# A graph layer with two hand-written orders: bucket ranks spread between the chunks of h, zero writes two per chunk, and a new order inside each unit of 20

## What is computed

```python
h = x @ W_in2f
Wij = (ssp(f_ij @ W_filt1 + b_filt1) @ W_filt2 + b_filt2) * rcut_ij[:, None]   # ssp: softplus - ln 2
agg = segment_sum(h[idx_j] * Wij, idx_i, num_segments=6250)
out = layernorm(x + ssp(agg @ W_out1 + b_out1) @ W_out2 + b_out2)
```

## Time and profile before

| | us |
|---|---|
| median of 3 runs | 2242.66 |
| lowest and highest run | 2235.79 and 2242.95 |
| time of the profiled execution | 2232.01 |
| its span, first to last instruction | 2230.1 |
| start of TensorE's first edge layer (line 1768) | 110.04 |
| first and last scatter (line 716) | 135.3 and 2138.7 |
| busy in the span: TensorE, VectorE, GpSimd, ScalarE | 2044.0, 1889.0, 1747.9, 1591.8 |

### The profile page before, as it was taken

One profiled execution on the slowest core, in us unless ns is written; L12 is line 12 of the kernel. 1 busy time (PEld: TensorE's weight loads), 2 busy tenths in 40 slices (PEclk: granted clock), 3 DMA queues, 4 the chain that ended last, 5 costly groups with the idle time before them and its releaser, 6 DMA issues.

```text
span 2230.1 us, 54072 instructions
## 1 busy us (share of the span) xinstructions
PE 2044.0 (92%) x15953; PEld 1681.7 (75%) x15953; DVE 1889.0 (85%) x3919; ACT 1591.8 (71%) x3812; POOL 1747.9 (78%) x1078
## 2 busy tenths in 40 slices
PE   3479999999999999999999999999999999999945
PEld 2357878787878778877878887788878787878733
DVE  6468989898989889988989898898989898989836
ACT  0278777777777777877778777777777777778616
POOL 2048888888888888888888888888888888888873
PEclk9589999999999999999999999999999999999978
DMA  6746666666666665656666656656666666666494
GB/s 234 279 85 104 94 94 96 101 101 88 99 99 89 98 98 94 95 90 106 98 90 100 95 93 100 99 94 94 97 100 97 91 100 96 92 97 96 55 234 128
DMA packets 353785, 239.34 MB, mean 107 GB/s; under 512 B 86919, under 2 KB 332786, under 8 KB 353338
## 3 DMA queue, kind: packets, MB, share of 16 engines
q0 software_dynamic: 146736, 66.85, 32.2%
q1 hardware_dynamic: 196326, 152.61, 27.1%
q10 hardware_dynamic: 10476, 16.77, 2.0%
HBM read 147.25 MB, written 88.83 MB: 106 GB/s over the span
## 4 chain that ended last, share of the span: by engine, by line
DMA 35%; PE 23%; POOL 16%; issue 15%; DVE 5%; ACT 3%; POOLq 0%; ACTq 0%; DVEq 0%; SPq 0%
DMA table<-total,index 33%; POOL table L716 16%; PE unit_psum L1824 6%; PE unit_psum L1843 4%; PE both_psum L1781 4%; PE total_psum L1794 3%; PE pre_psum L1768 2%; PE both_psum L1806 1%; PE both_psum L1777 1%; DMA h_parts<-h_out 1%; DMA b_o<-in_b_o 1%; ACT out_rows L1082 1%; ACT total L852 1%; DVE scat_hot L1377 1%; DVE route_hot L1360 1%
## 5 line engine op out<-in xcount | busy, mean ns | idle before, releaser
L716 POOL DMA_INDIRECT table<-total,index x1019 | 1689.2, 1658 | 428.9 <-issue 255.5
L1824 PE MATMUL unit_psum<-moving,route_hot 128*128 128x258 f32 x3808 | 602.7, 297 | 9.1 <-ACT ring L893 5.8
L1824 PEld LDWEIGHTS unit_psum<-moving,route_hot 128*128 128x128 f32 x3808 | 496.2, 191 | 72.3 <-ACT ring L893 51.4
L893 ACT ACTIVATE ring<-unit_psum 128x258 fp32r<-128x258 f32 x952 | 353.4, 394 | 245.6 <-PE unit_psum L1824 227.2
L869 ACT ACTIVATE h_dst<-both_psum,cols 128x128 f32<-128x128 f32 x1564 | 445.0, 373 | 96.5 <-PE both_psum L1806 95.1
L1843 PE MATMUL unit_psum<-scat_hot,ring 64*128 64x448 f32 x3808 | 461.1, 379 | 10.5 <-DVE scat_hot L1377 6.3
L1377 DVE TENSOR_SCALAR scat_hot<-node_iota,ring 128x448 fp32r<-128x448 uint16 x952 | 433.0, 474 | 9.1 <-ACT ring L893 5.0
L1781 PEld LDWEIGHTS both_psum<-w_f,hidden 128*128 128x128 f32 x3128 | 423.7, 196 | 11.6
L1781 PE MATMUL both_psum<-w_f,hidden 128*128 128x128 f32 x3128 | 421.6, 278 | 0.0
L1360 DVE TENSOR_SCALAR route_hot<-node_iota,cols 128x896 fp32r<-128x896 uint16 x544 | 378.9, 715 | 45.2 <-PE unit_psum L1824 44.2
L1843 PEld LDWEIGHTS unit_psum<-scat_hot,ring 64*128 64x128 f32 x3808 | 340.1, 185 | 89.3 <-ACT ring L893 30.3
(11 more groups left out here) (118 smaller groups left out, 1507.4 us busy)
## 6 DMA issues: line engine op xcount, KB each, us to landing
dst_b<-dst SPq DMA_DIRECT2D x391, 128.0 KB
src_b<-src SPq DMA_DIRECT2D x255, 128.0 KB, 3.4
f_t<-in_f_t SPq DMA_DIRECT2D x100, 256.0 KB, 3.6
table<-total,index POOLq DMA_INDIRECT x1019
table<-zeros ACTq DMA_DIRECT2D x20, 640.0 KB, 5.6
window<-h_parts SPq DMA_DIRECT2D x391, 32.0 KB
parts<-table SPq DMA_DIRECT2D x48, 256.0 KB, 5.0
h_parts<-h_out SPq DMA_DIRECT2D x12, 384.0 KB, 5.4
```

The lines of the kernel that those rows point to most:

```text
L716: pool.indirect_dma_start(tables[table], bass.IndirectOffsetOnAxis(index[:, i, k:k + 1], 0), total[:, i, k, 0:DIM], None, compute_op=ALU.a ...
L893: act.activation(ring[:, r[1] % RING, k, :], unit_psum[:, k % 2, 0:MOVING], ACT.Copy).then_inc(ring_done, 1)
L1824: last = pe.matmul(unit_psum[:, k % 2, 0:MOVING], route_hot[:, tile, k * P:(k + 1) * P], moving[:, tile, :], start=(tile == 0), stop=(tile ...
```

## The change

On all engines the loop over two chunks is unrolled, and the work on the routed edges stands between the chunks: on VectorE the bucket marks stand between chunks 1 and 4, the ranks between chunks 4 and 10, and `judge_windows` stands after the last subtraction of the high part, at the end. `count_in_buckets` is cut into one step per bucket, placed between the `node_features` of chunks 3 to 12. The diagonal of the triangular matrix `earlier` now holds 1024, so that an edge's own count carries a mark; a rank is then `max(rank, counts - 1024)`, one instruction per bucket in place of a product and a sum. SP issues the first loads of features, `dst` and `src` between the stores of h, and ScalarE writes two zeros after each of the chunks 2 to 6, one before each of the chunks 7 to 11, and one before each of the chunks 0 to 2. In the third stage VectorE takes `norm_shift` ahead of the clamp. In the second stage the same steps stand in another order on TensorE, ScalarE and VectorE; a unit now begins and ends about one pair of groups earlier in the pipeline. GpSimd's scatters are unchanged.

```diff
@@ SP
-            for quad in range(FEEDS):
-                load_features((0, quad))
-            sp.wait_ge(edges16_stored, 32)
-            for i in range(QUAD):
-                load_dst((0, i))
-                if plain(i):
-                    load_src((0, i), plain)
-
-            with sp.Fori(0, FULL_CHUNKS // 2 - 1) as j:
-                for b in range(2):
-                    load_x_t((j, b + 2), CHUNK // P)
-                    store_h((j, b), CHUNK // P)
+            for c in range(FULL_CHUNKS - 2):
+                load_x_t((0, c + 2), CHUNK // P)
+                store_h((0, c), CHUNK // P)
+                if 1 <= c <= FEEDS:
+                    load_features((0, c - 1))
+                if c == FEEDS:
+                    sp.wait_ge(edges16_stored, 32)
+                if FEEDS <= c < FEEDS + QUAD:
+                    load_dst((0, c - FEEDS))
+                    if plain(c - FEEDS):
+                        load_src((0, c - FEEDS), plain)
...
@@ GpSimd
             pool.affine_select(out=earlier[:, :], in_=earlier[:, :], compare_op=ALU.is_ge, fill=0.0, base=-1,
+                               pattern=[[1, P]], channel_multiplier=-1).then_inc(const_step, 1)
+            pool.wait_ge(const_step, 3)
+            pool.affine_select(out=earlier[:, :], in_=earlier[:, :], compare_op=ALU.not_equal, fill=OWN_MARK, base=0,
                                pattern=[[1, P]], channel_multiplier=-1).then_inc(consts_made, 1)
...
@@ ScalarE, split_h
-                if not isinstance(c[0], int):
-                    for k in range(1 + b, TABLES, 2):
-                        zero(k, c[0])
-                else:
-                    zero(0, min(2 + c[1], FIFTHS - 1))
+                if c[1] < FIFTHS - 2:
+                    zero(0, 2 + c[1])
+                elif 7 <= c[1] < 7 + FIFTHS:
+                    zero(2, c[1] - 7)
                 act.wait_ge(h_mm, after_chunk(c))
...
                 act.activation(h_out[:, b, 0:tiles, 1, :], h_rest[:, b, 0:tiles, :], ACT.Copy).then_inc(h_mid, 1)
-
-            run_chunks(act, split_h, LAST_H)
+                if 2 <= c[1] < 2 + FIFTHS:
+                    act.wait_ge(edges16_stored, 32)
+                    zero(1, c[1] - 2)
+                    zero(3, c[1] - 2)
+
+            for c in range(FULL_CHUNKS):
+                split_h((0, c), CHUNK // P)
+            split_h((0, FULL_CHUNKS), LAST_H // P)
...
@@ VectorE, ranks
-                for b in range(BUCKETS):
-                    dve.wait_ge(meta_mm, b + 1)
-                    part = rank[:, 0:ROUTES * TILES] if b == 0 else rank_part[:, :]
-                    counts = (both_psum if b % 2 else unit_psum)[:, :, 0:META_HALF * TILES]
-                    dve.wait_ge(meta_step, steps)
-                    dve.tensor_tensor(part.rearrange("p (h c) -> p h c", h=2), counts,
-                                      in_bucket[:, b, :].rearrange("p (h c) -> p h c", h=2), ALU.mult
-                                      ).then_inc(meta_step, 1)
-                    steps += 1
-                    if b:
-                        dve.wait_ge(meta_step, steps)
-                        dve.tensor_tensor(rank[:, 0:ROUTES * TILES], rank[:, 0:ROUTES * TILES], rank_part[:, :],
-                                          ALU.add).then_inc(meta_step, 1)
-                        steps += 1
+            def rank_in_bucket(b):
+                dve.wait_ge(meta_mm, b + 1)
+                counts = (both_psum if b % 2 else unit_psum)[:, :, 0:META_HALF * TILES]
+                ranks = rank[:, 0:ROUTES * TILES].rearrange("p (h c) -> p h c", h=2)
+                if b == 0:
+                    dve.tensor_scalar(ranks, counts, -OWN_MARK, 0.0, ALU.add, ALU.max).then_inc(meta_step, 1)
+                else:
+                    dve.wait_ge(meta_step, META_HOTS + b)
+                    dve.scalar_tensor_tensor(ranks, counts, -OWN_MARK, ranks, ALU.add, ALU.max).then_inc(meta_step, 1)
...
@@ VectorE, chunks of h (take_hi and take_mid are the two subtractions of split_h)
-            run_chunks(dve, split_h, LAST_H)
+            full = CHUNK // P
+            take_hi((0, 0), full)
+            make_order()
+            take_mid((0, 0), full)
+            take_hi((0, 1), full)
+            find_buckets()
+            take_mid((0, 1), full)
+            for b in range(4):
+                mark_bucket(b)
+            take_hi((0, 2), full)
...
+            take_mid((0, 3), full)
+            find_local()
+            take_hi((0, 4), full)
+            rank_in_bucket(0)
+            take_mid((0, 4), full)
+            rank_in_bucket(1)
+            rank_in_bucket(2)
+            for c in range(5, 11):
+                take_hi((0, c), full)
+                rank_in_bucket(2 * c - 7)
+                take_mid((0, c), full)
+                if c < 10:
+                    rank_in_bucket(2 * c - 6)
+            place_routed()
+            take_hi((0, 11), full)
+            make_biases()
+            take_mid((0, 11), full)
+            take_hi((0, FULL_CHUNKS), LAST_H // P)
+            judge_windows()
+            take_mid((0, FULL_CHUNKS), LAST_H // P)
...
@@ TensorE, chunks of h
-            run_chunks(pe, node_features, LAST_H)
+
+            for c in range(4):
+                node_features((0, c), CHUNK // P)
+            count_in_bucket(0)
+            count_in_bucket(1)
+            node_features((0, 4), CHUNK // P)
+            node_features((0, 5), CHUNK // P)
+            count_in_bucket(2)
+            node_features((0, 6), CHUNK // P)
+            for c in range(7, FULL_CHUNKS):
+                count_in_bucket(2 * c - 11)
+                count_in_bucket(2 * c - 10)
+                node_features((0, c), CHUNK // P)
+            for b in range(2 * FULL_CHUNKS - 11, BUCKETS):
+                count_in_bucket(b)
+            node_features((0, FULL_CHUNKS), LAST_H // P)
+            count_crowded()
...
@@ VectorE, last_layers
             def last_layers(i):
+                c = plus(i, -2)
+                if is_chunk(c):
+                    b, tiles = c[1] % 2, tiles_of(c)
+                    dve.wait_ge(e_inv, after_chunk(c))
+                    previous(dve, e_norm, c, after_chunk)
+                    dve.scalar_tensor_tensor(norm_shift[:, b, 0:tiles], mean_var[:, b, 0:tiles, 0], -1.0,
+                                             inv_dev[:, b, 0:tiles], ALU.mult, ALU.mult).then_inc(e_shift, 1)
+
                 c = i
...
-                c = plus(i, -2)
-                if is_chunk(c):
-                    b, tiles = c[1] % 2, tiles_of(c)
-                    dve.wait_ge(e_inv, after_chunk(c))
-                    previous(dve, e_norm, c, after_chunk)
-                    dve.scalar_tensor_tensor(norm_shift[:, b, 0:tiles], mean_var[:, b, 0:tiles, 0], -1.0,
-                                             inv_dev[:, b, 0:tiles], ALU.mult, ALU.mult).then_inc(e_shift, 1)
```

More of the change, by code:

```diff
@@ L951, in unit @@
                 soften_exp(pair(7))
+                weigh_h_dst(g(12), plain)
                 soften_ln(pair(7))
+                split_hi(r(3))
+                copy_total(g(9), plain)
                 weigh_h_dst(g(13), plain)
-                split_hi(r(3))
+                keep_slots(m(4), 0)
+                soften_abs(pair(8))
+                keep_slots(m(4), 1); keep_slots(m(4), 2)
+                soften_exp(pair(8))
+                copy_total(g(10), plain)
+                keep_slots(m(4), 3)
@@ L1212, in place_routed @@
+            def place_routed():
+                steps = META_HOTS + BUCKETS
                 assert steps == META_STEPS - 2
@@ L1435, in unit @@
+                route_one_hot(r(1), 2)
+                add_slice(m(2), 0)
+                route_one_hot(r(1), 3)
+                make_index(g(3), plain)
+                slot_one_hot(m(3), 0)
+                add_slice(m(2), 1)
+                slot_one_hot(m(3), 1)
+                finish_hidden(pair(4))
                 compare_src(g(7), plain)
-                add_slice(m(2), 0); add_slice(m(2), 1)
-                slot_one_hot(m(3), 0)
+                slot_one_hot(m(3), 2)
+                mark_repeated(g(4), plain)
@@ new lines, in unit @@
+                split_lo(r(2))
+                slot_one_hot(m(4), 0)
+                add_slice(m(3), 0); add_slice(m(3), 1)
+                multiply(g(10), plain)
+                finish_hidden(pair(6))
+                slot_one_hot(m(4), 1); slot_one_hot(m(4), 2); slot_one_hot(m(4), 3)
+                compare_dst(g(12))
+                slot_one_hot(m(4), 4); slot_one_hot(m(4), 5)
+                multiply(g(11), plain)
+                mark_repeated(g(7), plain)
+                make_index(g(7), plain)
@@ L1504, in unit @@
-                split_lo(r(4))
-                route_one_hot(r(4), 3)
                 add_slice(m(5), 0); add_slice(m(5), 1)
-                compare_src(g(15), plain)
+                make_index(g(12), plain)
+                slot_one_hot(m(6), 1); slot_one_hot(m(6), 2)
```

(32 more changed lines are left out.)

763 lines of the change are left out of this document (358 added, 405 removed).

## The result

The changed kernel takes 2229.85 us (median of 7 runs, 2222.32 to 2232.22), the kernel before 2238.14 beside it (7 runs, 2233.23 to 2242.95): a ratio of 0.9947, 95% interval 0.9929 to 0.9964. It is faster by 0.5%. The forecast was 2213 against 2242.66, 1.3%: the sign was right and the time lies in the range, but less than a third of the 30 us came.

A forecast was written before the change was run, and what follows sets the result against it. GpSimd's scatters were taken as the bound. From 2232.0 us, 24.0 off before the first edge layer, 0 for fill and scatters, and 6 off after the last gave 2202.0, or 2213 on the median's scale; range 2196 to 2235.

The forecast's parts named there:

- Three pieces, GpSimd the bound: Whole kernel: 135.3 us to the first scatter, 1018 GpSimd scatter steps of 2003.4 us, 91.4 us after the last.
- no unit ran dry: Second stage, rival at 0.13: the new order leaves GpSimd idle in every unit; at 3 us a unit, 2272 us.
- Chunks 2 to 4, done at 42.8: Prologue: these three chunks of h keep the old loop, 8.38 us for two, 12.6 us in all, ending at 42.8.
- The serial rest, 11.5 us: End of prologue: routing, window judging, biases, last two chunks' subtractions and issue behind the flag, one after another, 11.5 us.
- Chunks 5 to 10, 9.9 to 11.9 us for two: Prologue: a longer loop through loads, counts and ranks, 29.7 to 35.7 us in all, ending at 72.5 to 78.5.
- 5.23 from the issue of an `x_t` to its matmuls: Term of the prologue's loop over two chunks: from SP issuing the `x_t` load to TensorE's matmuls, 5.23 us.
- an inserted load: Term of the prologue's loop over two chunks: SP's issue of one load of features or `dst`, 0.92 us.
- the 86: End of prologue: TensorE's first edge layer starts at 86 us, from a range of 84.0 to 90.0, 24.0 us earlier.
- The floor by the bytes: Prologue: 5.4 MB in 20 us, then 23.0 MB at 393 GB/s in 58.5 us, so no earlier than 78.5.
- The transfers hold the chunks: Prologue, rival at 0.11: at 330 GB/s the bytes end at 89.7, first edge layer near 95, time 2217 us.
- The fill, 0 with bounds of 2: From first edge layer to first scatter, 25.3 us before: no change, bounds -2 and +2 us.
- Third piece, -6: Last scatter to end: `norm_shift` ahead of the clamp saves up to 0.7 us each; 6 us, bounds 0 and 7.5.

The follow-up runs named there:

- late_start_timed: The changed kernel with GpSimd's first scatter held until the third total is copied; ratio 0.9982 to the kernel before, where the changed kernel had 0.9961 on that chip.
- x4_timed: The changed kernel with four buffers for `x_t` in place of two, timed; 2222.34 us, ratio 0.9906 to the kernel before.
- x4: The changed kernel with four buffers for `x_t` in place of two, a single untimed execution; first edge layer at 92.78 us.
- order_only: The kernel before with only the new order of the units, prologue and last stage old; ratio 1.0059 to the kernel before, 1.0006 again on another chip.

## Why the prediction was wrong in size

- *Three pieces, GpSimd the bound*: right. The second piece is 2004.4 us for a forecast of 2003.4, no unit ran dry, and TensorE's 15.7 us of extra busy time changed nothing. A first scatter that is moved comes through to the end nearly whole: 8.9 us later are 7.5 us more in late_start_timed, 7.0 earlier 7.9 less in x4_timed.
- *Chunks 2 to 4, done at 42.8*: 43.66 + 0.69 = 44.35. *The serial rest, 11.5 us*: 101.16 - 90.48 = 10.7.
- *Chunks 5 to 10, 9.9 to 11.9 us for two*: this step failed. The loop was the right one, but the three rounds took 14.8, 17.9 and 13.4 us, 46.1 instead of 29.7 to 35.7. The term "5.23 from the issue of an `x_t` to its matmuls" measured 7.30, 9.46 and 6.97, together 8.0 us more; the store's issue and "an inserted load" came to 3.17, 3.80 and 1.50 for a forecast of 1.27, 4.7 us more, because two loads stood there in some rounds and each issue took 1.1 to 1.5 us in the first two rounds. (In the first round TensorE was busy up to the matmuls at 55.01, so part of its 7.30 is TensorE's own work.) The two terms are 12.7 of the 15.2 us between 86 and 101.16. The other terms of the loop, between their values at the two clocks, were 1.7 over what the 86 had for them, chunks 2 to 4 added 1.5, and the serial rest took 0.8 off.
- Behind both terms is one mistake: durations were read in a stretch in which SP inserted nothing, and then used where stores, features, `dst`, `src` and two zeros a chunk run together. The rate alone does not tell the two apart: the stretch that was read had the engines as full (1.02 and 393 GB/s) as 40 to 60 us here. What grew is the bytes of two chunks: three zeros and no inserted load before, 2 x (256 + 384) + 3 x 640 = 3200 KB, and four zeros and two inserted loads now, 4352 KB. The floor by the bytes was worked out for the whole prologue (78.5 us), where it did not bind. It comes close to binding for chunks 2 to 6, which have two zeros each: 256 + 384 + 256 + 2 x 640 KB are 2.2 MB, and at 372 GB/s 6 us a chunk, 12 of the 14.8 us of the first round.
- *The transfers hold the chunks*, the rival at 0.11, is what happened, by more than its price: its sign was a first layer near 95. Its rate was near, 321 GB/s from 25 to 90 us for its 330, and the loop was over at 90.48, where it had the bytes end at 89.7. Its price left out the serial rest of 10.7 us behind that.
- *The fill, 0 with bounds of 2*: 0.2 longer, and over its bound in another profile: 25.5 us in the first profile, 28.4 and 26.9 in two others of the same kernel.
- *Third piece, -6*: this step failed too: -1.4 (90.0, and 89.9 and 89.2 in two more profiles). The saving was taken as the clamp's 0.75 for each chunk, with the shift at its 0.15 wherever it stands. The 0.75 do come where GpSimd is idle (5.06 to 4.28 us a chunk); where it adds, the shift stands until the addition ends. So the loop gave 3.5 us and not 7.5, and the stretch ahead of it took 2.1 back. What lengthens that stretch is not shown; it has 29.6 to 32.4 us over all the runs, 30.6 and 30.9 in the two other profiles of this kernel. The Trainium skill has the rule (SBUF — State Buffer, section Who interferes with whom): a VectorE instruction with two inputs in SBUF contends with a GpSimd instruction that reads SBUF, for a port pair that it calls an exclusive lock. The trace agrees: the shift ends at 2178.35, the addition at 2178.33. I had cited that section for the scatters and not asked what it does to the one instruction that the change moves.

## What to carry to other kernels

A loop's transfer terms must be taken with the bytes that the change itself brings into it: sum the bytes per round, divide by the rate seen when the engines are full, and compare with the round. Where a prefetch has two buffers, a longer landing goes straight into the loop; a third and fourth buffer help only until the bytes of a round are the limit, and then moving bytes elsewhere is what is left. Before an instruction is moved, look at what the neighbour engine does at its new place, and at how many of its operands lie in SBUF.

## What the runs showed of the hardware

The fill goes by TensorE's clock. The same kernel (x4 and x4_timed) had fills of 25.54 and 28.82 us; the sums by stretch of the first, and then of the second:

```profile
105.00:110.00 5.00, 4.92 (x35) 3.66 (x36) 3.72 (x6) 4.39 (x11) 0.00 (x0) 1.00 0.26 80
```

```profile
105.00:110.00 5.00, 5.00 (x20) 3.14 (x20) 1.80 (x4) 2.67 (x6) 0.00 (x0) 0.50 0.21 60
```

The granted clock is 1.00 (2.4 GHz) in the one and 0.50 (1.2 GHz) in the other, after the same work, and the eight matmuls of `second_layer` there take 1.05 and 1.91 us. The fill of one kernel can thus differ by 3 us between executions; what lets the clock rise earlier in one is not shown.

The mean scatter step differs between chips and executions of the same kernel, with the shortest step always 1.84: 1.989 and 1.971 us in the two profiles of order_only, 18 us in all, more than the change itself won. A profile of one execution can't show a change of a few microseconds in that piece. A timed ratio on one chip is better but not safe: order_only's two, 1.0038 to 1.0079 and 0.9991 to 1.0022, do not meet.
